# Placing the split weights, the tokens and the hidden rows of a routed feed-forward layer at chosen byte offsets

## The reference

```
x = x + 0.5 * ffn(layernorm(x))        # top 2 of 8 experts, D = 256, F = 1024
x = x + attention(layernorm(x))        # linear attention, 16 heads of 16
x = x + 0.5 * ffn(layernorm(x))        # the same experts again

ffn: logits = x @ Wr; top 2 experts per token, softmax weights
     each expert takes at most CAP = 2560 tokens, in order of arrival
     h = silu(xe @ W1[e]) * (xe @ W3[e]);  ye = h @ W2[e]
     out[token] += weight * ye
```

## Time and profile before

| | |
|---|---|
| median of 3 executions | 2962.55 us (2958.39 to 2963.34) |
| the profiled execution, first to last instruction | 2957.9 us |
| TensorE busy, share of the span | 95% |
| VectorE, ScalarE, GpSimd busy | 54%, 44%, 39% |
| matmuls, and weight loads | 18643 each |
| granted TensorE clock, mean | 0.979 |

### The profile page before, as it was taken

The page is one execution under the profiler, slowest core; times in us unless marked ns, Lnnn a source line. Parts: engine busy times, 40 slices in busy tenths (PEclk is TensorE's granted clock), DMA queues, the critical chain, the costliest instruction groups (busy, mean ns, idle before and its releaser), DMA issues.

```text
span 2957.9 us, 54694 instructions
## 1 busy us (share of the span) xinstructions
PE 2823.4 (95%) x18643; PEld 2528.6 (85%) x18643; DVE 1595.3 (54%) x3765; ACT 1297.3 (44%) x2765; POOL 1165.2 (39%) x1550
## 2 busy tenths in 40 slices
PE   4499999999999999989999995999999999999999
PEld 3389899989999989878888885998999998899988
DVE  8754545445454545447878875444545454445453
ACT  5543434444344434334444444444434343444443
POOL 3754434444444434311111113453444443444533
PEclk8799999999999999999999997999999999999999
DMA  7552323232332312221121014223323231323212
GB/s 253 190 127 37 79 37 79 43 80 38 83 70 47 86 33 40 35 58 36 54 71 46 31 45 121 59 43 76 83 38 79 43 86 30 81 42 80 43 29 34
DMA packets 155114, 197.23 MB, mean 67 GB/s; under 512 B 15536, under 2 KB 127024, under 8 KB 154928
## 3 DMA queue, kind: packets, MB, share of 16 engines
q0 software_dynamic: 62688, 87.11, 17.9%
q1 hardware_dynamic: 81952, 97.30, 10.1%
q10 hardware_dynamic: 10288, 10.38, 1.0%
HBM read 124.32 MB, written 78.79 MB: 69 GB/s over the span
## 4 chain that ended last, share of the span: by engine, by line
PE 54%; DVE 1%; ACT 0%; issue 0%; DMA 0%; POOL 0%; DVEq 0%; ACTq 0%; POOLq 0%
PE e_ps L100 8%; PE e_ps L101 8%; PE e_ps L102 8%; PE e_psy L1203 5%; PE mi_qk L1458 4%; PE e_ps L1203 3%; PE e_psy L1205 3%; PE mi_sc L1474 2%; PE mi_yo L1494 2%; PE mi_xv L1464 2%; PE mi_yo L1521 2%; PE e_ps L1205 2%; PE mi_kv L1508 1%; PE mi_yo L1482 1%; PE e_psx L1189 1%; PE mi_qk L1515 0%
## 5 line engine op out<-in xcount | busy, mean ns | idle before, releaser
L1306 DVE TENSOR_TENSOR e_h_lo<-e_hid,e_h_hi 128x384 fp32r<-128x384 f32 (+1 forms) x640 | 384.1, 600 | 399.3 <-ACT e_h_hi L1267 392.5
L1303 DVE TENSOR_TENSOR e_hid<-e_ps,e_gate 128x384 f32<-128x384 f32 (+1 forms) x640 | 381.7, 596 | 372.6 <-ACT e_gate L1263 359.3
L1267 ACT ACTIVATE e_h_hi<-e_hid 128x384 fp32r<-128x384 f32 (+1 forms) x640 | 356.8, 558 | 423.2 <-DVE e_hid L1303 416.7
L1263 ACT ACTIVATE e_gate<-e_ps 128x384 f32<-128x384 f32 (+1 forms) x640 | 333.8, 522 | 407.0 <-PE e_ps L102 397.8
L100 PE MATMUL e_ps<-e_xT_hi,e_wb 128*128 128x384 f32 (+1 forms) x1280 | 456.3, 357 | 0.0
L102 PE MATMUL e_ps<-e_xT_hi,e_wb 128*128 128x384 f32 (+1 forms) x1280 | 455.0, 355 | 0.0
L101 PE MATMUL e_ps<-e_xT_lo,e_wb 128*128 128x384 f32 (+1 forms) x1280 | 455.0, 355 | 0.0
L100 PE MATMUL e_ps<-e_xT_hi,c_wa 128*128 128x384 f32 (+1 forms) x1280 | 450.7, 352 | 2.5 <-DVE e_xT_lo L1295 2.5
L102 PE MATMUL e_ps<-e_xT_hi,c_wa 128*128 128x384 f32 (+1 forms) x1280 | 449.1, 351 | 0.0
L101 PE MATMUL e_ps<-e_xT_lo,c_wa 128*128 128x384 f32 (+1 forms) x1280 | 448.9, 351 | 0.0
L461 POOL DMA_INDIRECT c_xrow<-normed_rows,e_token x320 | 347.2, 1085 | 153.2 <-POOL e_token L1092 76.9
(11 more groups left out here) (302 smaller groups left out, 4735.7 us busy)
## 6 DMA issues: line engine op xcount, KB each, us to landing
c_raw<-w SPq DMA_DIRECT2D x204, 256.0 KB
normed_rows<-r_xn SPq DMA_DIRECT2D x8, 1056.0 KB, 6.9
normed_rows<-mi_xn SPq DMA_DIRECT2D x8, 1056.0 KB, 4.8
x<-x ACTq DMA_DIRECT2D x8, 1024.0 KB, 12.1
out<-mi_x SPq DMA_DIRECT2D x8, 1024.0 KB, 5.3
r_xin<-x SPq DMA_DIRECT2D x7, 1024.0 KB, 11.0
c_raw<-x SPq DMA_DIRECT2D x7, 1024.0 KB, 9.1
c_xrow<-normed_rows,e_token POOLq DMA_INDIRECT x320
```

Source lines behind the costliest of these rows:

```text
L1263: act.activation(gate[:, f % 2, 0:n], ps1[f % 2][:, 0:n], ACT.Silu).then_inc(gated, 1)
L1267: act.activation(h[0][:, f, 0:n], hid[:, f % 2, 0:n], ACT.Copy).then_inc(h_high, 1)
L1303: dve.tensor_tensor(hid[:, f % 2, 0:n], ps3[f % 2][:, 0:n], gate[:, f % 2, 0:n], ALU.mult).then_inc(hid_ready, 1)
L1306: dve.tensor_tensor(h[1][:, f, 0:n], hid[:, f % 2, 0:n], h[0][:, f, 0:n].bitcast(F32), ALU.subtract).then_inc(h_ready, 1)
```

## The change

Three things are placed anew. An unused buffer of 512 bytes ahead of `c_wa` and one of 480 bytes ahead of `e_wb` make both slots begin at a multiple of 1024 bytes. An unused buffer of 288 bytes ahead of `xT_hi` does the same for `xT`, `gate`, `hid`, `h` and `yrow`. Each slot is made 128 numbers (512 bytes) longer, and an expert's split weights, high and low behind each other as before, begin at an offset inside the slot that depends on the phase and the expert: in the first expert phase 0, 4, 8, 12, 16, 24, 32 and 48 bytes for experts 0 to 7, in the second 64, 96, 128, 192, 256, 320, 384 and 512 bytes. The split of each expert's weights and the matmuls use that offset; `behind(e)` names the phase and the expert for which a slot is being filled. The entry (0,) for a third phase serves the copy that the last expert of the last phase makes. No instruction is added, removed or moved, and no size or shape of an operand changes. Everything that lies behind `c_wa` and isn't named here moves by exactly 1024 bytes, or lies behind `e_wb` and moves by another multiple of 32.

```
+SPACE_A, SPACE_B, SPACE_X = 128, 120, 72
+SHIFTS = ((0, 1, 2, 3, 4, 6, 8, 12), (16, 24, 32, 48, 64, 80, 96, 128), (0,))
+ROOM = 128
...
+def split_weights(slot, phase, e):
+    at = SHIFTS[phase][e]
+    return slot[:, at:at + 2 * WCOLS].rearrange("p (u c) -> p u c", u=2)
...
+        first_w = split_weights(slot_a, 0, 0)
...
-                    act.activation(piece(slot_a[:, 0], q), piece(raw, q), ACT.Copy).then_inc(w_high, 1)
+                    act.activation(piece(first_w[:, 0], q), piece(raw, q), ACT.Copy).then_inc(w_high, 1)
...
-        slot_b = m.sb("wb", [P, 2, WCOLS], F32R)
+        m.sb("space_b", [P, SPACE_B])
+        slot_b = m.sb("wb", [P, 2 * WCOLS + ROOM], F32R)
...
+        m.sb("space_x", [P, SPACE_X])
         xT = [m.sb("xT_hi", [P, KD, WIDE], F32R), m.sb("xT_lo", [P, KD, WIDE], F32R)]
...
+        def behind(e):
+            return (phase, e + 1) if e + 1 < E else (phase + 1, 0)
...
-                    both = slots[s]
+                    both = split_weights(slots[s], phase, e)
...
-                    act.activation(piece(slots[1 - s][:, 0], q), piece(raw, q), ACT.Copy).then_inc(w_high, 1)
+                    high = split_weights(slots[1 - s], *behind(e))[:, 0]
+                    act.activation(piece(high, q), piece(raw, q), ACT.Copy).then_inc(w_high, 1)
...
-                    dve.tensor_tensor(piece(slots[1 - s][:, 1], q), piece(raw, q), piece(slots[1 - s][:, 0], q).bitcast(F32),
+                    both = split_weights(slots[1 - s], *behind(e))
+                    dve.tensor_tensor(piece(both[:, 1], q), piece(raw, q), piece(both[:, 0], q).bitcast(F32),
                                       ALU.subtract).then_inc(w_low, 1)
...
-        slot_a = m.sb("wa", [P, 2, WCOLS], F32R)
+        m.sb("space_a", [P, SPACE_A])
+        slot_a = m.sb("wa", [P, 2 * WCOLS + ROOM], F32R)
```

More of the change, by code:

```diff
@@ L861, in low_w @@
                     dve.wait_ge(w_high, q + 1)
-                    dve.tensor_tensor(piece(slot_a[:, 1], q), piece(raw, q), piece(slot_a[:, 0], q).bitcast(F32),
+                    dve.tensor_tensor(piece(first_w[:, 1], q), piece(raw, q), piece(first_w[:, 0], q).bitcast(F32),
                                       ALU.subtract).then_inc(w_low, 1)
@@ L908, in _ @@
                             pool.wait_ge(w_high, q + 1)
-                            pool.tensor_tensor(piece(slot_a[:, 1], q), piece(raw, q), piece(slot_a[:, 0], q).bitcast(F32),
+                            pool.tensor_tensor(piece(first_w[:, 1], q), piece(raw, q), piece(first_w[:, 0], q).bitcast(F32),
                                                ALU.subtract).then_inc(w_low, 1)
```

## The result

The changed kernel takes 2972.23 us (2970.87 to 2972.54) against 2962.36 us (2958.39 to 2963.34): ratio 1.0039, 95% interval 1.0027 to 1.0051. The medians differ by 9.9 us, the ratio gives 11.6 us. In the profiled executions the span goes from 2957.9 to 2969.2 us. From the first transpose of the first expert phase to the start of its last tile it was 1257.73 - 146.11 = 1111.62 us and is 1264.77 - 147.14 = 1117.63 us, 6.0 us more. From the second phase's second tile to its last one it was 1081.97 us and is 1086.71, 4.7 us more. All but 0.6 us of the longer span lies in these two stretches.

What follows compares the result with a forecast made beforehand. The prediction took TensorE's matmul start distances to bound the kernel, running without gaps in both expert phases. Its terms, each taken as 0, summed to 0 on the 2962.6 us median, rounded to 2963; range 2925 to 3000.

Steps and rivals of the forecast that it cites:

- What bounds the kernel: Both expert phases, 76% of the span: time is the number of matmuls times the distance of their starts.
- The step of about 6 ns: TensorE's SBUF reads: 5.9 ns per 512-column first-product matmul, 6.4 ns per pair, between `c_wa` and `e_wb`; together 58.8 us.
- The opposite sign of the two products: `e_wb` against `c_wa`: 512-column first-product matmuls 5.9 ns slower, second-product pairs 6.4 ns faster.
- Alignment: Slots and tokens at multiples of 1024: taken as 0, bounds -58.8 or +58.8 us on all matmuls.
- Rival B: Tokens and weights starting 0 instead of 256 bytes apart spare a meeting of streams: 2904, 2918 or 2943 us; chance 0.24.
- C: Tokens and weights beginning in the same place slow all matmuls, even in expert 0: 3022 us; chance 0.07.
- Offsets per expert: Sixteen weight offsets in the slots replace two: taken as 0, bounds -14.1 and +13.0 us.
- the two classes persist: All tiles stay like `c_wa` or `e_wb`, nothing measurable changes: 2963 us, own range 2949 to 2976; chance 0.43.
- Short offsets: Six experts' weights at no multiple of 32 bytes: taken as nothing, upper bound +22.1 us.
- rival A: Weights off the grid lengthen distances in first-phase experts 1 to 5 and 7: 2977 or 2985 us; chance 0.22.
- Writing at short offsets: VectorE's and ScalarE's split-weight pieces, 682 and 625 ns: taken as 0; VectorE 10% slower would be 8.7 us.
- Rival D: VectorE or ScalarE writes split weights slower at short offsets: 2966 us at 10%, 2996 us at twice the time; chance 0.04.

Runs made afterwards that it cites:

- `tokens_4`: Changed kernel with `xT` and `h` starting 4 bytes off a multiple of 256, weights at 0 in the first phase, 4 bytes in the second: 3010.82 us, one execution.
- `tokens_low_128`: Changed kernel with every expert's weights at offset 0 and the low tokens moved 128 bytes: 2976.66 us, one execution.

## Why the prediction was right, and where it was not

**What bounds the kernel: right.** The gaps in the earlier trace rows, 1.4 us of 1137, lie at the start of the first phase, and after an expert's first tile TensorE never waits; only the distance of the starts changed. That TensorE sees the slots' places was read from the earlier trace rows and held in the changed kernel and the nine run since. The step of about 6 ns was a difference of two tiles' means. Inside a tile single distances differ by 7 to 11 ns (173 and 180, 350 and 361), and the means move by any part of that. The opposite sign of the two products holds between 0 and 32 bytes, but not everywhere: at 4 and 24 bytes both are longer than at 0. And "353.2 ns from `c_wa`" was not the slot's only value even then:

```profile
176.53:210.30 33.77, 33.77 (x171) 28.65 (x170) 14.21 (x22) 12.72 (x22) 15.84 (x21) 1.00 0.52 137
```

This is a big tile from `c_wa` in the kernel before, with pairs at 346.8 ns and 0.23 us less than the 34.00 of the earlier trace rows.

**Alignment: right.** Taken at 0 with 1.6 us of gain when all tiles become like `c_wa`; alone it gave 0.1%, with an interval from 0.01 to 0.19%, and 1.6 us in the tiles. The argument that multiples of 512 can't matter held; so do multiples of 256, which it left open. Rival B (a common start saves a step, 0.24) and C (it costs one, 0.07) fell: the difference of -256 bytes in `c_wa` was already the same as 0.

**Offsets per expert: the term that failed.** The prediction took "the two classes persist" and 0 us, with +13.0 as its worst. There are more than two classes. The eight offsets of the second phase, all of them multiples of 32, add 4.7 us, read from the starts: 5.8 us in experts 0 to 6, less 1.1 us that expert 7 gains by going from 544 bytes to 512, which counts like 0. 64, 96, 128, 320 and 384 bytes give a first product of 174.7 to 176.7 ns in small tiles, a mean that neither slot had shown, and W2 at 64 or 320 bytes pays 352.4 to 353.4 ns a pair while the first product pays 233. Two offsets, 512 and 544, were too few to call what they gave the only classes; small tiles seemed not to react because both samples happened to lie where they don't. The forecast's own condition, 173 to 174 ns in every small tile, is what broke.

**Short offsets: nothing taken, up to +22.1 us allowed.** Experts 1 to 5 and 7 of the first phase add 5.5 us (expert 6, at 32 bytes, 0.5 more). That is a quarter of rival A (0.22), whose sign, longer distances in these experts, came true in part. Its reason isn't shown by it: multiples of 32 such as 96 and 128 lengthen small tiles as much (176.7 and 176.0 ns), 12 bytes cost nothing in the pairs, 4 bytes a full step, and 8, 16 and 48 nothing in most small tiles' first product. Only `tokens_4` parts the short offset from the distance, for 4 bytes alone, and there the cost is real (with everything 4 bytes off, +6.7 ns with 384 columns, +10.4 with 512, +6.9 on a pair). The Trainium skill, "SBUF — State Buffer", Door 1, has reads of SBUF in lines of 16 bytes and a price for each crossing; the slow remainder 4 fits, the fast remainder 12 doesn't, so the rule alone doesn't give the curve.

**Writing at short offsets: right.** VectorE's and ScalarE's pieces into `e_wb`, which held 4, 12, 24 and 48 bytes in the first phase, after, to be set beside the earlier trace rows:

```profile
L1267 ACT ACTIVATE e_wb<-c_raw x96: 620/626/635, 154.2 to 2692.5; 128x512 fp32r<-128x512 f32 x96
L1308 DVE TENSOR_TENSOR e_wb<-c_raw,e_wb x96: 674/683/739, 156.0 to 2694.2; 128x512 fp32r<-128x512 f32 x96
```

The medians are 626 and 683 ns, and taken expert by expert none is over 628 and 686. Rival D is out.

**The numbers.** 2963 was forecast and 2972.2 measured, inside the range (2925 to 3000) and inside the likeliest case's own range (2949 to 2976). By the prediction's own measure of 0.2% the kernel did get slower, so the single value missed the sign. The chance for "slower", 0.39, was the largest of the three; the point stayed with "no change", 0.31. Two mis-sized terms, both taken as 0, make up the 10.7 us of the two stretches: 5.2 us for the offsets that are multiples of 32, 5.5 us for the shorter ones. That the result lies inside 2949 to 2976 is partly luck: the upper end, +13.0 us, was worked out for two classes, and there are more.

**What stays open.** Why a step exists, and which two reads meet. Distance decides at 0 and 64 bytes for the first product, a common start 4 bytes off costs more than one at 0, and the same addresses can run in two ways (16 bytes: 25.65 and 25.94 us). Which way isn't chance: in two of these kernels it is the same tile of every expert. In the first phase of `tokens_4` the second small tile behind the big ones has 173.5 ns and its neighbours 178.4; in `tokens_low_128` the first big tile takes 34.58 us and the next 34.37. That is like two streams of reads that fall into step with each other, one way or the other by how the tile began, but this is a guess; no run here isolates the mechanism. Why no matmul costs less than 13 ns over its columns was not found either.

## What to carry to other kernels

Where TensorE runs without gaps, read the distance of starts in a long row of equal matmuls, for each buffer by itself; if two buffers that do the same differ by nanoseconds, their places are a tuning knob. Scan it with many offsets in one run, tile by tile, before calling two samples "the classes", and read each product by itself: the offset that is best for one product was a slow one for the other, and only separating them (0 for W1 and W3, 32 bytes for W2) gained 0.5%. Keep moving operands on 16-byte starts unless a scan says otherwise.

## What the runs showed of the hardware that was not expected

- The distance of back-to-back `fp32r` matmuls depends on where the stationary and the moving buffer start, for multiples of 64 bytes with a period of 256: 173.4 to 180.1 ns with 384 columns, 226.8 to 237.7 with 512, 346.5 to 360.7 for a pair of 512 and 256 (means over a tile).
- Inside a tile the distances follow a short cycle, such as 173 and 180 ns in turn, or 349, 350 and 361 ns a pair.
- Moving both operands of the first product by 64 bytes restores the fast distance (226.9 ns); moving both by 4 bytes doesn't (237.7 ns).
- At some offsets the same instructions at the same addresses settle at one of two distances for a whole tile: 173.5 or 176.7 ns at 16 bytes, 353 or 347 ns a pair at 0.
